# Maximum and sum over the slots on VectorE instead of TensorE, and the next octet's tokens turned at the head of chunk 1

## The reference

```python
x = layernorm(layernorm(x)) ; se = layernorm(slot_embeds) * scale
logits = einsum('bnd,esd->bnes', x, se)
dispatch = softmax(logits, axis=1)                     # over the tokens of a sequence
combine = softmax(logits.reshape(b, n, E * S), axis=-1)  # over all 1024 slots
slots = einsum('bnd,bnes->besd', x, dispatch)
eout = (gelu(slots @ Wg + bg) * (slots @ Wu + bu)) @ Wd + bd
out = einsum('bns,bso->bno', combine, eout)            # x = x + tanh(g) * out
```

## Time and profile before

| | |
|---|---|
| median of three runs | 1505.92 us |
| profiled execution | 1507.57 us |
| its span, first to last instruction | 1505.90 us |
| TensorE products busy | 1382.3 us, 92% |
| VectorE busy | 953.9 us, 63% |
| ScalarE busy | 1013.6 us, 67% |
| GpSimd busy | 524.3 us, 35% |
| granted TensorE clock, mean | 0.981 |

### The profile page before, as it was taken

The page is one execution under the profiler, slowest core; times in us unless marked ns, Lnnn a source line. Parts: engine busy times, 40 slices in busy tenths (PEclk is TensorE's granted clock), DMA queues, the critical chain, the costliest instruction groups (busy, mean ns, idle before and its releaser), DMA issues. The chain is left out here.

```text
span 1505.9 us, 33716 instructions
## 1 busy us (share of the span) xinstructions
PE 1382.3 (92%) x12029; PEld 1174.7 (78%) x12029; DVE 953.9 (63%) x2374; ACT 1013.6 (67%) x2019; POOL 524.3 (35%) x510
## 2 busy tenths in 40 slices
PE   5898699899999999999999999988999999877895
PEld 4887588788888888888888888876788888655673
DVE  6998766766766767677667666543455555644455
ACT  5887587577676776776776767647788888534442
POOL 3112355322322323223223223212235555545553
PEclk9999899999999999999999999999999999979998
DMA  8300100499930000000000000040000000122236
GB/s 222 85 1 1 58 2 1 87 183 84 114 17 2 2 1 2 2 2 1 2 2 1 2 2 2 1 114 15 1 31 15 16 16 19 31 63 69 70 92 175
DMA packets 124980, 60.46 MB, mean 40 GB/s; under 512 B 41945, under 2 KB 120241, under 8 KB 124690
## 3 DMA queue, kind: packets, MB, share of 16 engines
q1 hardware_dynamic: 120274, 48.92, 18.4%
q0 software_dynamic: 4544, 9.38, 1.9%
HBM read 28.84 MB, written 29.44 MB: 39 GB/s over the span
## 5 line engine op out<-in xcount | busy, mean ns | idle before, releaser
L1349 DVE SCALAR_TENSOR_TENSOR hidden<-psU,b_cols,gelu 128x512 f32<-128x512 f32 x256 | 191.6, 750 | 170.5 <-ACT gelu L1474 95.6
L1474 ACT ACTIVATE gelu<-psG,b_cols 128x512 f32<-128x512 f32 x256 | 176.5, 689 | 110.1 <-PE psG L142 97.2
L1296 POOL TENSOR_TENSOR combine_sum<-combine_sum,combineT 128x512 f32<-128x512 f32 x48 | 63.4, 1322 | 294.7 <-ACT combineT L1488 294.7
L1325 POOL TENSOR_TENSOR dispatchT<-dispatchT,dispatch_inv 128x512 f32<-128x512 f32 x64 | 67.8, 1060 | 232.5 <-DVE dispatch_inv L1453 232.5
L1608 PE MATMUL psU<-w_down,hidden 128*64 128x128 f32 x2048 | 123.4, 273 | 0.0
L1608 PE MATMUL psDown<-w_down,hidden 128*64 128x128 f32 x2048 | 122.7, 273 | 0.0
L1861 POOL TENSOR_TENSOR probs<-probs,row_sum 128x512 f32<-128x512 f32 x64 | 66.4, 1037 | 143.5 <-DVE row_sum L1974 142.6
L1608 PEld LDWEIGHTS psU<-w_down,hidden 128*64 128x64 f32 x2048 | 113.2, 137 | 1.3 <-issue 1.2
L1608 PEld LDWEIGHTS psDown<-w_down,hidden 128*64 128x64 f32 x2048 | 113.9, 137 | 0.1
L140 PE MATMUL psG<-slots_hi,w_gate_hi 128*128 128x512 f32 x256 | 106.4, 416 | 0.5 <-DVE slots_lo L1435 0.5
L2038 ACT ACTIVATE probs<-psS,neg_max 128x128 f32<-128x128 f32 x256 | 91.4, 385 | 22.8 <-DVE neg_max L1971 16.8
(11 more groups left out here) (406 smaller groups left out, 3624.8 us busy)
## 6 DMA issues: line engine op xcount, KB each, us to landing
sorted_x<-empty_rows SPq DMA_DIRECT2D x1, 12736.0 KB, 76.5
tile_rows<-sorted_x SPq DMA_DIRECT2D x78, 65.0 KB
sorted_x<-empty_rows SPq DMA_DIRECT2D x1, 4544.0 KB, 30.3
expert_ys<-expert_y SPq DMA_DIRECT2D x16, 256.0 KB, 3.7
x<-in_x SPq DMA_DIRECT2D x8, 256.0 KB, 5.9
ctx<-in_ctx SPq DMA_DIRECT2D x8, 256.0 KB, 5.9
w_gate_raw<-in_L_ffn_Wg SPq DMA_DIRECT2D x1, 2048.0 KB, 10.6
w_up_raw<-in_L_ffn_Wu SPq DMA_DIRECT2D x1, 2048.0 KB, 15.8
```

The source lines that it names most:

```text
L1325: pool.tensor_tensor(e[:], e[:], over(rb[:], SEQ, 2), ALU.mult).then_inc(s["eb_normed"], 1)
L1349: dve.scalar_tensor_tensor(hid[e][:, half, :], U[half][:], bcol[:, 1, 4 * ch + 2 * e + half:][:, 0:1], gel[half][:], ALU.add, ALU.mult).th ...
L1474: act.activation(gel[half][:], G[half][:], ACT.Gelu, bias=bcol[:, 0, 4 * ch + 2 * e + half:][:, 0:1]).then_inc(s["gelu"], 1)
```

## The change

The maximum and the sum over the slots leave TensorE. VectorE turns the 128x512 array in blocks of 32x32 (`dve.transpose`), reduces each block over its free axis, which leaves a maximum (or sum) for each quadrant of 32 partitions, copies quadrants 1 to 3 beside quadrant 0, and reduces over the four. The maxima are then copied to all four quadrants and turned back with a broadcast, which gives `mb`. The sums are copied to `ra`, laid out by token. `max_quadrants` runs at the end of chunk 6 and `max_rows` at the head of chunk 7; in front of the first octet both run in its chunk 7, ahead of slots_lo. `sum_quadrants` runs in chunk 7 ahead of the first expert_out, `sum_inverse` behind slots_lo. The score product of chunk 7 moves to chunk 6. The next octet's tokens are turned behind the dispatch transposes at the head of chunk 1, into the second half of `psM`.

```diff
-    AHEAD = ((), (), (0,), (1, 2), (3,), (4, 5), (6,), (7,))
+    AHEAD = ((), (), (0,), (1, 2), (3,), (4, 5), (6, 7), ())
+    Q = P // 32
...
+            def by_quadrant(source, turned, n, op, count):
+                dve.transpose(turned[:], source).then_inc(s[n + "_turned"], 1)
+                need(dve, s[n + "_turned"], count)
+                dve.tensor_reduce(quad[n][:, 0, :], turned[:].rearrange("p (b i) -> p b i", i=32), AX.X, op
+                                  ).then_inc(s[n + "_quad"], 1)
+            def together(n, out, done, op, count):
+                need(dve, s[n + "_quad"], count)
+                for q in range(1, Q):
+                    last = dve.tensor_copy(quad[n][0:32, q, :], quad[n][32 * q:32 * (q + 1), 0, :])
+                last.then_inc(s[n + "_together"], 1)
+                need(dve, s[n + "_together"], count)
+                dve.tensor_reduce(out, quad[n][0:32].rearrange("p q b -> p b q"), AX.X, op).then_inc(s[done], 1)
+                need(dve, s[done], count)
+            def max_quadrants(o):
+                need(dve, s["lb_max"], 8 * (o + 2))
+                need(dve, s["ct_sub"], 8 * (o + 1))
+                need(dve, s["mtok"], o + 1)
+                by_quadrant(top[:], mb, "max", ALU.max, o + 2)
+            def max_rows(o):
+                need(dve, s["mb_ready"], o + 1)
+                together("max", mtok[0:32, :], "mtok", ALU.max, o + 2)
+                for q in range(1, Q):
+                    last = dve.tensor_copy(mtok[32 * q:32 * (q + 1), :], mtok[0:32, :])
+                last.then_inc(s["max_spread"], 1)
+                need(dve, s["max_spread"], o + 2)
+                dve.transpose(mb[:].rearrange("p (b i) -> p b i", i=32), over(mtok[:], 32, 2)).then_inc(s["mb_ready"], 1)
+            def sum_quadrants(o):
+                need(dve, s["ct_summed"], 7 * (o + 1))
+                need(dve, s["max_turned"], min(o + 2, OCTETS))
+                need(dve, s["dtok"], o)
+                by_quadrant(total[:].rearrange("p t n -> p (t n)"), top, "sum", ALU.add, o + 1)
+            def sum_inverse(o):
+                need(dve, s["den"], o)
+                together("sum", dtok[0:32, :], "dtok", ALU.add, o + 1)
+                need(dve, s["x_new"], o)
+                for q in range(Q):
+                    last = dve.tensor_copy(ra[32 * q:32 * (q + 1), :],
+                                           dtok[0:32, :].rearrange("p (t q) -> p t q", q=Q)[:, :, q])
+                last.then_inc(s["den"], 1)
+                need(dve, s["den"], o + 1)
+                dve.reciprocal(ra[:], ra[:]).then_inc(s["den_inv"], 1)
+                need(dve, s["den_inv"], o + 1)
+                dve.tensor_scalar(ra[:], ra[:], c.gates[:, 1:2], None, ALU.mult).then_inc(s["den_gated"], 1)
... VectorE's body
                     if has_core(o) and exists(o, ch, -1):
                         expert_out(k - 1, 1, (ch - 1) % CH)
+                    if ch == CH - 1 and has_head(o) and has_core(o):
+                        max_rows(o)
+                    if ch == 1 and has_head(o) and has_core(o):
+                        need(dve, s["lnT_hi"], o + 1)
+                        need(dve, s["lb"], 8 * (o + 1))
+                        dve.tensor_tensor(lnT[1][:], M[:, 1, :], lnT[0][:].bitcast(F32), ALU.subtract
+                                          ).then_inc(s["lnT_lo"], 1)
...
                     if has_core(o):
+                        if ch == CH - 1:
+                            sum_quadrants(o)
                         expert_out(k, 0, ch)
-                    if ch == CH - 1 and has_head(o):
-                        need(dve, s["top_t"], o + 2)
-                        need(dve, s["mb"], o + 1)
-                        dve.tensor_reduce(mtok[:], G0, AX.X, ALU.max).then_inc(s["mtok"], 1)
+                    if ch == CH - 1 and has_head(o) and not has_core(o):
+                        max_quadrants(o)
+                        max_rows(o)
... behind slots_lo
+                    if has_core(o) and has_head(o) and ch == CH - 2:
+                        max_quadrants(o)
                     if has_core(o) and ch == CH - 1:
-                        need(dve, s["den"], o + 1)
-                        need(dve, s["x_new"], o)
-                        dve.reciprocal(ra[:], U[0][:, 0:OP]).then_inc(s["den_inv"], 1)
-                        need(dve, s["den_inv"], o + 1)
-                        dve.tensor_scalar(ra[:], ra[:], c.gates[:, 1:2], None, ALU.mult).then_inc(s["den_gated"], 1)
+                        sum_inverse(o)
... ScalarE's body, ahead of the gelus
+                    if ch == 1 and has_head(o) and has_core(o):
+                        need(act, s["tx"], o + 1)
+                        need(act, s["lb"], 8 * (o + 1))
+                        act.copy(lnT[0][:], M[:, 1, :]).then_inc(s["lnT_hi"], 1)
... behind slots_hi
-                        act.copy(lnT[0][:], G[1][:]).then_inc(s["lnT_hi"], 1)
-                    if ch == CH - 1 and has_head(o):
-                        act.copy(mb[:], G[1][:]).then_inc(s["mb_ready"], 1)
... TensorE's body, behind dispatch_turned
+                    if ch == 1 and has_head(o) and has_core(o):
+                        need(pe, s["x_normed"], o + 1)
+                        need(pe, s["sl_lo"], 2 * (k + 1))
+                        for t in range(OP):
+                            last = pe.transpose(M1[:, t, :], xn[1 - par][:, t, :], c.ident[:])
+                        last.then_inc(s["tx"], 1)
... ahead of the slots product
+                        if ch == 1 and has_head(o) and has_core(o):
+                            need(pe, s["lnT_lo"], o + 1)
... around the second down product
-                            last = pe.transpose(G1[:, t, :], xn[1 - par][:, t, :], c.ident[:])
-                            last = pe.transpose(G0[:, t, :], top[:, t * P:(t + 1) * P], c.ident[:])
-                            last = pe.matmul(U[0][:, t:t + 1], total[:, t, :], ones[:], start=True, stop=True)
-                            last = pe.matmul(G[1][:, t * P:(t + 1) * P], mtok[:, t:t + 1].to_broadcast([P, P]), ident_r[:],
```

More of the change, by code:

```diff
@@ L1208, in stage_experts0 @@
         top = sb("top_over_chunks", [P, OT])
-        mtok, mb = sb("max_c", [P, OP], F32R), sb("max_c_row", [P, OT])
-        ident_r = sb("ident_rounded", [P, P], F32R)
+        quad = {n: sb(f"{n}_by_quadrant", [P, Q, OT // 32]) for n in ("max", "sum")}
+        mtok, mb = sb("max_c", [P, OT // 32]), sb("max_c_row", [P, OT])
+        dtok = sb("sum_c", [P, OT // 32])
         eb = [sb(f"dispatchT{i}", [P, OB, SEQ]) for i in range(2)]
@@ L1226, in stage_experts0 @@
         M = c.bank(ctx, "psM", [P, 2, 512], 2)
-        G0 = G[0][:].rearrange("p (t s) -> p t s", t=OP)
-        G1 = G[1][:].rearrange("p (t s) -> p t s", t=OP)
+        M1 = M[:, 1, :].rearrange("p (t s) -> p t s", t=OP)
         U1 = U[1][:].rearrange("p (t s) -> p t s", t=OP)
         DOWN = (DN[:], U1)
-        names = ("bd_loaded rows_loaded ones_ready ident_r aggr inv_a inv_b inv_done b_t b_ready "
-                 "x_hat x_scaled x_normed tx lnT_hi lnT_lo lb lb_max raw top_t mtok mb mb_ready "
+        names = ("bd_loaded rows_loaded ones_ready aggr inv_a inv_b inv_done b_t b_ready "
+                 "x_hat x_scaled x_normed tx lnT_hi lnT_lo lb lb_max raw max_turned max_quad max_together mtok max_spread mb_ready "
                  "shifted eb_exp eb_sum eb_inv eb_normed td d_ready sl sl_hi sl_lo ct_sub ct_ready ct_summed "
-                 "w_hi w_lo den den_inv den_gated gate up gelu hidden down eo_ready combined x_new bn")
+                 "w_hi w_lo sum_turned sum_quad sum_together dtok den den_inv den_gated gate up gelu hidden down eo_ready combined x_new bn")
         s = {n: sem("b_" + n) for n in names.split()}
@@ L1292, in sum_combine @@
                 if ch == 1:
-                    need(pool, s["den"], o)
+                    need(pool, s["sum_turned"], o)
                 else:
@@ L1467, in _ @@
             act.wait_ge(s["ones_ready"], 1)
-            act.copy(ident_r[:], c.ident[:]).then_inc(s["ident_r"], 1)
             def gelu(k, e, ch, half):
@@ L1579, in gate_up @@
                 cols = slice(half * P, (half + 1) * P)
-                first = isinstance(k, int) and ch == 0 and e == 0
-                if first:
-                    need(pe, s["mtok"] if half == 0 else s["mb_ready"], k // CH + 1)
-                if ch == 2 and e == 0 and half == 1 and k // CH < OCTETS - 1:
-                    need(pe, s["lnT_lo"], k // CH + 1)
+                if isinstance(k, int) and k == 0 and e == 0:
+                    pe.wait_ge(s["raw"], CH)
                 need(pe, s["gelu"], q - 1)
                 product3(pe, G[half][:], [w[:, 2 * ch + e, cols] for w in wg], x).then_inc(s["gate"], 1)
-                if first and half == 0:
-                    need(pe, s["den_inv"], k // CH)
                 if e == 0 and half == 1:
```

34 lines of the change are left out of this document (1 added, 33 removed).

## The result

The changed kernel takes 1534.63 us (median of 4 runs, 1533.33 to 1538.61), beside 1506.26 for the kernel before on the same chip: a ratio of 1.0191, interval 1.0177 to 1.0206. The profiled execution has a span of 1531.5 us, 25.6 more than before. Predicted was 18.2 more; the medians say 28.4 more. The direction and the places are right, the size is 10 us short: 1534.63 lies above the forecast's own range (1515 to 1531) and inside the wide one (1508 to 1537).

The account below looks back on a forecast made before the run. TensorE is 92% busy, but VectorE's chain was taken to bind the seam. Terms 17.0 + 0.1 + 2.1 - 0.7 - 0.3 = +18.2 us; forecast 1524 against the median 1505.92, own range 1515 to 1531.

Parts of the forecast that it names:

- the forecast's own range: Whole kernel: 1515 to 1531 us around the forecast of 1524, given a chance of 0.52.
- the wide one: Whole kernel: the range meant to hold 8 in 10, 1508 to 1537 us, reaching into neighbouring rivals.
- the 2.31: Chunk 7: 2.31 us of TensorE work that the change takes out, forecast to bring no gain at seams with x_hat.
- Chunk 7: Ahead of hidden(0,0): 3.81 us of added VectorE delay, less 0.95 idle and 1.03 room, stalls TensorE 1.83 us.
- The chain into chunk 0: VectorE from chunk 7's first down product to chunk 0's hidden: 7.54 + 1.60 - 0.60 = 8.54 us, so +1.00.
- A seam: Passage between octets whose chunk 0 has x_hat: 1.83 + 1.00 = 2.83 us more, six times, 17.0 us.
- First octet: Before any expert work: 3.31 us of maxima work on VectorE's chain makes slots_lo 2.06 us later, +2.1.
- Last octet: Its column sums (1 us) go and 1.60 us of VectorE work comes in; expert_out had waited 1.46: -0.3 us.
- the seam ahead of it: Seam before the last octet, without x_hat: 1.83 stalled, 2.31 saved, expert_out 0.6 us late; in sum +0.1 us.
- Tokens: Turning the tokens at the head of chunk 1 instead of its tail: 0.1 us gained, seven times, -0.7.
- dearer small operations and turnings: Small VectorE operations at 0.28 and turnings at 1.2 us: 3.9 to 5.1 a seam, +25 to +32, 1531 to 1538.
- rival (a): Chunk 0: TensorE's clock falls in the longer stand, five seams at 2.4 us, +12 on top, 1536; chance 0.18.

Follow-up runs that it names:

- the best kernel: Changed kernel with maxima spread over chunk 7, GpSimd's shifts in chunk 7, tiles at old bytes, all the sums' work after sum_quadrants in chunk 0: 1491.97 us, ratio 0.9900.
- the kernel with all moves: Changed kernel with maxima spread over chunk 7, sums' copies back, reciprocal and gate in chunk 0, GpSimd's shifts in chunk 7, tiles at old bytes: 1495.40 us, ratio 0.9922.

## Why the prediction was right in its mechanism and short in its size

- **VectorE binds the seam, and none of the 2.31 is kept:** right. TensorE's idle time ahead of psU grew from 5.0 to 33.7 us, and the best kernel shows the 2.31 appear once VectorE's chain is out of the way.
- **Chunk 7:** a stall of 1.83 forecast, 1.50 measured. The added VectorE work is 1.34 (806.48 to 807.82) and 2.42 (809.33 to 811.75) = 3.76, forecast 3.81. The first three copies took 0.91 beside GpSimd, 0.39 over the 0.52 of the sums' (0.5 taken), and the small operations 0.17 to 0.28 (0.20 taken). But the bracket counts only from the modelled end of the product before. Chunk 7 is 13.68 - 11.81 = 1.87 longer than a plain chunk, and spreading the maxima gave 1.89 back: as a cost, the 1.83 was right.
- **The chain into chunk 0:** 8.54 forecast, 818.35 to 826.93 = 8.58 measured; x_hat 3.44 (3.47 forecast). TensorE waits 0.53 and 2.35, forecast about 0.6 and 2.7.
- **A seam:** chunks 6, 7 and 0 take 42.11 against 38.96, +3.15; less three times 0.10 for the place, +2.85. Forecast 2.83. So in five seams; in that of octets 0 and 1, of which the prediction says that "it shifts alike", the three take 48.26 against 46.01, so +1.95, 0.9 less.
- **First octet:** +2.1 forecast, about +2.3 measured: from the subtraction in front of it to slots_lo 4.08 us (174.64 to 178.72) against 1.85, and 0.1 more, beside the place, up to chunk 1. **Last octet:** from the head of its chunk 1 to the last output product -0.3 beside the place, as forecast; the seam ahead of it +0.6 beside the place instead of +0.1 (TensorE waits 0.68 there for expert_out, 0.6 forecast, and chunk 0 grew by 1.09).
- **Tokens:** 0.1 a chunk was taken. With tiles at the old bytes chunk 1 takes 12.11 against 12.39: -0.28, seven times -2.0. That the new place of the turning alone does it was not tried.
- **What was missed, the term that is not in the sum:** "A chunk is all TensorE" was taken to mean that untouched chunks keep their length. The prediction has no term for the place of the tiles, though the diff adds some; it costs 64 x 0.11 = 7.0 us. It is a cost that the products' own rate pays, and no wait shows it. None of the ranges holds it either: above 1531 the prediction had dearer small operations and turnings, which did not come (3.76 us for 3.81), and rival (a), which gave only 1.5 us. That 1534.63 still lies inside 1508 to 1537 is luck.
- **Rival (a)** came true in one seam, at +1.5 rather than 2.4, and so had a part beside the forecast, not in its stead.

The sum anew: 5 x 2.85 + 1.95 + 0.6 + 2.3 - 2.0 - 0.3 + 7.0 + 1.5 = 25.3, against 25.6 between the spans. That it closes so well is in part chance, since single terms are known to 0.1 or 0.2 and some count fivefold. The 28.4 between the medians holds 2 to 3 us that the two profiled executions don't show; the one after is the fastest of its four, the one before (1507.57) slower than its median.

## What to carry to other kernels

Work that leaves the busiest engine pays only where that engine's next wait isn't already set by another: read the chain at the seam before counting busy time, and put new VectorE work, piece by piece, where each consumer has room. Where a GpSimd pass runs beside short VectorE ones, move it before judging these. And when a change adds tiles, compare a stretch that it doesn't touch: a difference there may be the placement, which a pad alone in the old kernel tests, and should be taken out before anything else is explained.

## What the runs showed of the hardware

- The distance between the gate and up products depends on where the kernel's tiles lie: a plain chunk of the kernel before takes 11.68 us, 11.81 when its tiles stand 96 bytes on, with nothing else changed, and 11.68 again at 256 and at 512 bytes. The score, down, slots and combine products keep their distance.
- The granted clock after waits of 0.53 and 2.35 us some 1.7 us of products apart fell in one of five seams of the changed kernel, in one with it moved by 32 bytes, in three with the maxima spread and in four with the tiles at their old bytes, and the same wait of 2.37 us passed without a fall in the fifth. Where only one wait of 1.26 us stood, it fell in none. A fall cost 1.5 us.
- Three 32x16 copies take 0.52 us alone and 0.91 to 1.52 beside a GpSimd tensor_tensor. The one that meets it ends 0.02 to 0.03 us after it, the others take 0.16 as alone. VectorE's turning and its reduction of 128x512 are not stretched: in the kernel with all moves they take 0.70 and 0.69 (785.37 and 786.11) while GpSimd's shifts run (784.90 to 787.43).
- Queued 32x16 copies start 0.08 us apart within a quadrant and 0.18 across.
- VectorE's turning of 128x512 f32 takes 0.70 us, like the f32 reduction of the same tile (0.69).
